# A gated cross-attention block with experts: the last two tiles' steps in another order and on other banks

## The reference

```python
x = x + tanh(g_xattn) * xattn(layernorm(x), ctx, ctx, mask, ...)
x = x + tanh(g_ffn) * ffn(layernorm(x), ...)
# ffn(y):
attn_out = softmax(causal(q @ k.T * scale)) @ v @ out_proj_w.T + out_proj_b
x1 = layer_norm(y + attn_out, ln1_w, ln1_b)                 # "u" in the kernel
gates = softmax(x1 @ gate_w.T + gate_b)
top_gates, top_idx = top 2 of gates
moe_out = sum over the two of gate * (x1 @ expert_w[e].T + expert_b[e])
return layer_norm(x1 + moe_out, ln2_w, ln2_b)               # "v" in the kernel
```

## Time and profile before

| | |
|---|---|
| median of 3 runs | 829.06 us |
| profiled execution, whole | 831.21 us |
| its span from the first to the last instruction | 829.5 us |
| mean granted TensorE clock | 0.994 of 2.4 GHz |
| instructions | 24325 |
| TensorE busy | 779.7 us, 94% of the span |
| VectorE busy | 667.5 us, 80% |
| ScalarE busy | 564.4 us, 68% |
| GpSimd busy | 473.0 us, 57% |

### The profile page before, as it was taken

One profiled execution on the slowest core, in us unless ns is written; L12 is line 12 of the kernel. 1 busy time (PEld: TensorE's weight loads), 2 busy tenths in 40 slices (PEclk: granted clock), 3 DMA queues, 4 the chain that ended last, 5 costly groups with the idle time before them and its releaser, 6 DMA issues.

```text
span 829.5 us, 24325 instructions
## 1 busy us (share of the span) xinstructions
PE 779.7 (94%) x9515; PEld 611.9 (74%) x9515; DVE 667.5 (80%) x1908; ACT 564.4 (68%) x1268; POOL 473.0 (57%) x854
## 2 busy tenths in 40 slices
PE   8888989999999999999999999999999999999896
PEld 4465768777787787778787788778778777777663
DVE  5756668797978979797988979797988979787876
ACT  5786767777786777777776777678677777764320
POOL 8434535566665646566574646566564655555343
PEclk9999999999999999999999999999999999999999
DMA  7510000010100101010100101010010000000000
GB/s 202 159 39 16 2 17 16 8 37 9 37 8 2 37 8 36 9 36 9 29 16 2 38 8 37 8 37 9 10 35 2 9 8 8 9 8 8 8 7 20
DMA packets 33570, 20.75 MB, mean 25 GB/s; under 512 B 11672, under 2 KB 33456, under 8 KB 33456
## 3 DMA queue, kind: packets, MB, share of 16 engines
q1 hardware_dynamic: 33456, 19.19, 8.1%
HBM read 14.99 MB, written 4.19 MB: 23 GB/s over the span
## 4 chain that ended last, share of the span: by engine, by line
PE 56%; ACT 24%; DVE 14%; issue 4%; POOL 1%; DMA 0%; SPq 0%; DVEq 0%; POOLq 0%
PE bank L395 26%; PE bank L516 8%; PE bank L535 7%; ACT bank L776 6%; DVE neg_max_A L1022 6%; ACT bank L785 5%; DVE moe L1131 4%; ACT probs_B L826 3%; PE bank L556 3%; PE bank L585 3%; ACT probs_A L826 3%; PE bank L574 2%; PE bank L404 2%; ACT k_heads_B L809 2%; PE bank L546 1%
## 5 line engine op out<-in xcount | busy, mean ns | idle before, releaser
L1343 POOL TENSOR_SCALAR_AFFINE_SELECT probs_B<-probs_B 128x512 f32<-128x512 f32 x128 | 77.3, 640 | 184.4 <-ACT probs_B L826 184.4
L1131 DVE SCALAR_TENSOR_TENSOR moe<-bank,gates,moe 128x256 f32<-128x256 f32 x256 | 123.2, 481 | 48.2 <-PE bank L395 33.2
L785 ACT ACTIVATE bank<-mask_add 128x512 f32<-128x512 bf16 x128 | 76.6, 602 | 49.2 <-DVE neg_max_A L1022 49.2
L395 PE MATMUL bank<-w_expertsa,u_t_a 128*128 128x512 f32 x256 | 105.6, 413 | 0.1
L395 PE MATMUL bank<-w_expertsa,u_t_b 128*128 128x512 f32 x256 | 100.9, 394 | 0.0
L395 PE MATMUL bank<-w_expertsb,u_t_a 128*128 128x512 f32 x256 | 100.9, 394 | 0.0
L1022 DVE TENSOR_REDUCE neg_max_A<-bank 128x4 f32<-128x512 f32 x128 | 79.5, 684 | 11.9 <-PE bank L516 11.5
L1022 DVE TENSOR_REDUCE neg_max_B<-bank 128x4 f32<-128x512 f32 x128 | 79.3, 682 | 5.5 <-PE bank L516 5.5
L776 ACT ACTIVATE bank<-mask_add 128x512 f32<-128x512 bf16 x128 | 69.8, 626 | 0.0
L776 ACT ACTIVATE bank<-causal_add 128x512 f32<-128x512 bf16 x128 | 69.7, 623 | 0.0
L826 ACT ACTIVATE probs_A<-bank 128x512 f32<-128x512 f32 x128 | 66.1, 603 | 4.4 <-PE bank L556 2.2
(11 more groups left out here) (224 smaller groups left out, 2440.5 us busy)
## 6 DMA issues: line engine op xcount, KB each, us to landing
x_in<-in_x SPq DMA_DIRECT2D x32, 128.0 KB, 2.2
ctx_t<-in_ctxT SPq DMA_DIRECT2D x32, 128.0 KB, 2.2
out<-y_out SPq DMA_DIRECT2D x32, 128.0 KB, 1.7
w_stage<-in_expertsT SPq DMA_DIRECT2D x8, 256.0 KB, 4.3
mask_u<-in_masks SPq DMA_DIRECT2D x32, 32.0 KB, 2.1
w_stage<-in_in_projT SPq DMA_DIRECT2D x3, 256.0 KB, 4.8
w_stage<-in_WkT SPq DMA_DIRECT2D x1, 256.0 KB, 3.5
w_stage<-in_WvT SPq DMA_DIRECT2D x1, 256.0 KB, 3.6
```

Of the source, the lines that this page charges most:

```text
L395: done = pe.matmul(out_ap, l, r, start=n == 0, stop=n == len(terms) - 1)
L785: act.activation(score_banks[g][:].rearrange("p (h k) -> p h k", k=P), mask_add[t % MASK_SLOTS][:, 1:2, :].to_broadcast([P, GROUP, P]), AC ...
L1131: dve.scalar_tensor_tensor(out=moe[(e + 1) % 2][:], in0=bank[:, (e % 2) * EMBED:(e % 2 + 1) * EMBED], scalar=gates[:, e:e + 1], in1=moe[e ...
L1343: pool.affine_select(out=part, in_=part, compare_op=ALU.is_ge, fill=0.0, base=0, pattern=[[0, GROUP], [1, P]], channel_multiplier=-1).then ...
```

## The change

1. A table `LATE` gives six uses of the last tiles a score bank (0 to 3) in place of a work bank: `B_normalise`, `B_o_t`, `B_out`, `u_t` and `gate` of tile 31 and `pair3` of tile 29. They wait for the last exponentials of layer B (`B_exp`), or for nothing more than the steps before them do. `work_last` passes over these uses.
2. `u_transposed` waits for `u` only, in every tile; the wait for its bank's last reader is gone. ScalarE's copy of `u_t` waits, for tiles 30 and 31, for the last expert pair of the tile before.
3. TensorE in round 17: `normalise`, `o_transposed` and `project_o` of tile 31 go in between and behind the pairs of tile 29, five `keep_busy` matmuls go. Round 18: pairs 0 and 1 of tile 30 stand ahead of `transpose_gates(30)`, `u_transposed(31)` ahead of pair 3; `keep_busy` has 6 for 4 and 4 for 8 matmuls.
4. VectorE in round 18: `apply_u(30)`, tile 31's division and `o_t_B_b`, and `u_t_b(30)` go in between the sums of tile 29; the gates of tile 30 go ahead of `statistics("2", 29)`; `statistics("1", 31)` and its mean go into them. `apply_v(29)` goes behind `gates_low(30)`, and `bias_sum(30)` waits for it. Round 19: `u_t_b(31)` goes ahead of the last two sums of tile 30, and the gates of tile 31 ahead of `statistics("2", 30)`.
5. ScalarE takes `B_o_t` of tile 31 ahead of `u_t` of tile 30. GpSimd makes `u` of tiles 30 and 31 ahead of `finish` of tiles 28 and 29.

The diff at its core:

```diff
@@ -235,8 +235,15 @@
         def live(t):
             return 0 <= t < tiles
 
+
+        LATE = {("B_normalise", tiles - 1): (0, "B_exp", GROUPS * tiles), ("B_o_t", tiles - 1): (1, "B_exp", GROUPS * tiles),
+                ("B_out", tiles - 1): (2, "B_exp", GROUPS * tiles), ("pair3", tiles - 3): (3, "B_exp", GROUPS * tiles),
+                ("u_t", tiles - 1): (0, "B_on", tiles), ("gate", tiles - 1): (1, "B_ot_b", tiles)}
+
         def work_bank(use, n):
 
+            if (use, n) in LATE:
+                return score_banks[LATE[use, n][0]]
             key = (use, None) if (use, None) in WORK_AT else (use, n % PAIR)
             return work_banks[WORK_USES[WORK_AT[key]][2]]
 
...
-                _, half, other_bank, behind, readers = WORK_USES[turn % len(WORK_USES)]
+                other, half, other_bank, behind, readers = WORK_USES[turn % len(WORK_USES)]
                 pair = turn // len(WORK_USES) - behind
-                if other_bank == bank and live(PAIR * pair):
+                if other_bank == bank and live(PAIR * pair) and (half is None or (other, PAIR * pair + half) not in LATE):
...
         def tensor_program(pe):
             def take_work(use, t):
+                if (use, t) in LATE:
+                    pe.wait_ge(sem[LATE[use, t][1]], LATE[use, t][2])
+                    return work_bank(use, t)
                 for name, value in work_last(use, t):
                     pe.wait_ge(sem[name], value)
                 return work_bank(use, t)
...
-                transpose_two(take_work("u_t", t), u[t % U_SLOTS], "u_t", t)
+                transpose_two(work_bank("u_t", t), u[t % U_SLOTS], "u_t", t)
...
@@ TensorE, the round's steps
+                if r != 18:
+                    project_o("B", 2 * r - 5)
                 attend("B", 2 * r - 4)
                 scores("A", 2 * r - 1)
                 if r == 18:
-                    keep_busy("gates_t", 30, 4)
+                    keep_busy("gates_t", 30, 6)
+                if r == 18:
+                    expert_pair(0, 2 * r - 6)
+                if r == 18:
+                    expert_pair(1, 2 * r - 6)
                 transpose_gates(2 * r - 6)
-                expert_pair(0, 2 * r - 6)
+                if r != 18:
+                    expert_pair(0, 2 * r - 6)
                 expert_bias_sum(2 * r - 6)
-                expert_pair(1, 2 * r - 6)
+                if r != 18:
+                    expert_pair(1, 2 * r - 6)
                 expert_pair(2, 2 * r - 6)
...
                 normalise("B", 2 * r - 4)
+                if r == 18:
+                    u_transposed(2 * r - 5)
                 expert_pair(3, 2 * r - 6)
                 o_transposed("B", 2 * r - 4)
...
-                    keep_busy("pair0", 31, 8)
+                    keep_busy("pair0", 31, 4)
...
+                if r == 17:
+                    normalise("B", 2 * r - 3)
                 expert_pair(1, 2 * r - 5)
...
+                if r == 17:
+                    o_transposed("B", 2 * r - 3)
...
+                if r == 17:
+                    u_transposed(2 * r - 4)
+                if r == 17:
+                    project_o("B", 2 * r - 3)
                 project_q_b(r - 1)
-                if r == 17:
-                    keep_busy("u_t", 30, 5)
-                normalise("B", 2 * r - 3)
-                u_transposed(2 * r - 4)
+                if r != 17:
+                    normalise("B", 2 * r - 3)
+                if r != 17:
+                    u_transposed(2 * r - 4)
...
+                if use == "u_t" and t >= tiles - 2:
+                    act.wait_ge(sem[read[0]], read[1] * t)
                 act.activation(dst[0][:], work_bank(use, t)[:, 0:EMBED], ACT.Copy).then_inc(sem[name + "_a"], 1)
...
+                if t == tiles - 2:
+                    dve.wait_ge(sem["vn"], t)
...
@@ VectorE, rounds 18 and 19
+                if r == 19:
+                    low_part("u_t", u_t, "u_t", 2 * r - 7)
                 expert_sum(6, 2 * r - 8)
                 apply_x(2 * r - 1)
                 expert_sum(7, 2 * r - 8)
+                if r == 19:
+                    gate(2 * r - 7)
+                if r == 19:
+                    gate_rank(2 * r - 7)
+                if r == 19:
+                    gate_choice(2 * r - 7)
                 statistics("2", 2 * r - 8)
                 mean_variance("2", 2 * r - 8)
                 low_part("B_o_t", o_t["B"], "B_ot", 2 * r - 6)
...
+                if r == 18:
+                    apply_u(2 * r - 6)
                 bias_sum(2 * r - 7)
                 max_parts("A", 2 * r - 2)
                 expert_sum(0, 2 * r - 7)
                 expert_sum(1, 2 * r - 7)
+                if r == 18:
+                    inverse_sums("B", 2 * r - 5)
+                if r == 18:
+                    normalise("B", 2 * r - 5)
                 expert_sum(2, 2 * r - 7)
                 expert_sum(3, 2 * r - 7)
                 if r == 2:
                     split_low("E6")
                     split_low("E7")
                 low_part_of_pair("rope_t", rope_t, "rope_t", 2 * r - 3)
-                apply_u(2 * r - 6)
+                if r != 18:
+                    apply_u(2 * r - 6)
+                if r == 18:
+                    low_part("B_o_t", o_t["B"], "B_ot", 2 * r - 5)
                 expert_sum(4, 2 * r - 7)
                 expert_sum(5, 2 * r - 7)
+                if r == 18:
+                    low_part("u_t", u_t, "u_t", 2 * r - 6)
                 expert_sum(6, 2 * r - 7)
                 expert_sum(7, 2 * r - 7)
+                if r == 18:
+                    gate(2 * r - 6)
+                if r == 18:
+                    finish_b(2 * r - 5)
+                if r == 18:
+                    gate_rank(2 * r - 6)
+                if r == 18:
+                    statistics("1", 2 * r - 5)
+                if r == 18:
+                    mean_variance("1", 2 * r - 5)
+                if r == 18:
+                    gate_choice(2 * r - 6)
                 statistics("2", 2 * r - 7)
                 mean_variance("2", 2 * r - 7)
-                inverse_sums("B", 2 * r - 5)
-                normalise("B", 2 * r - 5)
...
+                if r == 18:
+                    apply_u(2 * r - 5)
                 gates_low(2 * r - 6)
-                mean_variance("1", 2 * r - 5)
+                if r != 18:
+                    mean_variance("1", 2 * r - 5)
                 apply_y(2 * r - 2)
                 maxima("A", 2 * r - 1)
+                if r == 18:
+                    apply_v(2 * r - 7)
                 bias_sum(2 * r - 6)
                 expert_sum(0, 2 * r - 6)
                 expert_sum(1, 2 * r - 6)
...
@@ GpSimd, round 19
+                if r == 19:
+                    scale_shift_u(2 * r - 8)
                 finish(2 * r - 10)
                 base_b(2 * r - 7)
-                scale_shift_u(2 * r - 8)
+                if r != 19:
+                    scale_shift_u(2 * r - 8)
...
```

More of the change, by code:

```diff
@@ L1159, in vector_program @@
                 low_part("y_t", y_t, "y_t", 2 * r - 5)
-                low_part("u_t", u_t, "u_t", 2 * r - 7)
+                if r != 19:
+                    low_part("u_t", u_t, "u_t", 2 * r - 7)
                 maxima("B", 2 * r - 5)
@@ L1221, in vector_program @@
                 apply_x(2 * r)
-                low_part("u_t", u_t, "u_t", 2 * r - 6)
-                apply_v(2 * r - 7)
-                low_part("B_o_t", o_t["B"], "B_ot", 2 * r - 5)
+                if r != 18:
+                    low_part("u_t", u_t, "u_t", 2 * r - 6)
+                if r != 18:
+                    apply_v(2 * r - 7)
+                if r != 18:
+                    low_part("B_o_t", o_t["B"], "B_ot", 2 * r - 5)
                 mean_variance("A", 2 * r + 1)
@@ L1233, in vector_program @@
                 mean_variance("B", 2 * r - 2)
-                gate_rank(2 * r - 6)
-                gate_choice(2 * r - 6)
-                finish_b(2 * r - 5)
+                if r != 18:
+                    gate_rank(2 * r - 6)
+                if r != 18:
+                    gate_choice(2 * r - 6)
+                if r != 18:
+                    finish_b(2 * r - 5)
                 if r == 0:
@@ L1240, in vector_program @@
                 low_part_of_pair("x_t", xn_t, "xn", 2 * r)
-                statistics("1", 2 * r - 5)
+                if r != 18:
+                    statistics("1", 2 * r - 5)
+                if r == 18:
+                    apply_u(2 * r - 5)
                 gates_low(2 * r - 6)
-                mean_variance("1", 2 * r - 5)
+                if r != 18:
+                    mean_variance("1", 2 * r - 5)
                 apply_y(2 * r - 2)
                 maxima("A", 2 * r - 1)
+                if r == 18:
+                    apply_v(2 * r - 7)
                 bias_sum(2 * r - 6)
@@ L1250, in vector_program @@
                 expert_sum(2, 2 * r - 6)
-                apply_u(2 * r - 5)
+                if r != 18:
+                    apply_u(2 * r - 5)
```

(5 more changed lines are left out.)

28 lines of the change are left out of this document (20 added, 8 removed).

## The result

| | before | after |
|---|---|---|
| median, same chip | 829.14 us (829.02 to 831.9, 7 runs) | 832.37 us (831.01 to 833.45, 7 runs) |
| ratio | | 1.0032 (95% interval 1.0021 to 1.0043) |
| profiled execution, span | 831.21, 829.5 | 832.29, 830.6 |
| granted clock in it | 0.994 | 0.996 |

What follows compares the result with a forecast made beforehand. TensorE, 94% busy, bounds the middle; the last 20 us are a chain of waits through GpSimd, VectorE and TensorE. Tile 31's bias matmul moves from 817.63 to 818.21, so 829.06 + 0.58 = 829.6 us; range 827.3 to 831.4.

Steps and rivals of the forecast that it cites:

- v_n: VectorE's apply_v(30) ahead of gates_low(31), meeting GpSimd's addition: 0.73 us taken, 0.40 with GpSimd quiet.
- Cost one: TensorE, tile 29: transposes directly behind the bias matmul wait for ScalarE's copy; 1.05 us, of which 0.47 only moved.
- Cost two: Ahead of tile 30's bias matmul: two GpSimd roots in a row, 1.69 us, leave TensorE 1.8 us idle.
- Cost three: Tile 30's statistics, mean, root and apply_v ahead of gates_low(31): last bias matmul at 818.21 against 817.63.
- The early gates: VectorE's gates of tile 31 were to come at 815.67 against 816.56, 0.9 us early.
- The parts priced at nothing: Wait taken from u's transposes (0 taken, 2.8 us at most), bank addresses, idle matmuls, ScalarE's added wait: no effect.
- The first, early gates carrying through: Rival: apply_v(30) doesn't hold gates_low and the end is 828.2, or 826.5 to 827.4 with the issue; chance 0.27.
- The second, the clock: Rival: TensorE's clock halves behind the new waits of 1.8 and about 1.4 us; 830.6, 831.0 or 832; chance 0.23.
- The third, nothing seen: Rival: losses some tenths smaller cancel with the gain, 829.1; within the forecast's own spread, 828.9 to 830.3.

Runs made afterwards that it cites:

- before filled more: Kernel before with two pairs of idle matmuls in TensorE's waits near 800 and five more near 746.7: 829.1 us, ratio 0.9989.
- the run with 15 waits: Changed kernel with both statistics moved back, TensorE's waits filled, plus 15 met semaphore waits in VectorE's tile 20: 830.85 us, ratio 1.0013.
- the filled kernels: Kernels with idle matmuls in TensorE's waits, among them before with two pairs (829.16 us), before with five more (829.1), the changed kernel (831.14).

## Why the prediction was wrong, point by point

**The step that failed** is the first sentence of the sum: "It is made on the span's axis of the profiled execution (829.5 us of its 831.21) and put on the median, 829.06, as a difference." The old order stood in it with a half-clock stretch inside the compared piece (tile 29 to tile 30: 13.44 us, 793.78 to 807.22), the new one at full clock (13.89 reckoned, 13.99 in the trace). At full clock the old one takes 12.18, and as far as tile 31's bias matmul 22.73 where the forecast had 23.85. So the difference of the first piece was put at 0.45 and is 1.80. I had the row that shows it and used it for a rival, not for the baseline. The 2.2 us between the profiled execution and the median were the same hint, two steps of 1.1. The end of that piece in the trace of before:

```profile
807.22 0.28 PE L611 MATMUL bank<-expert_bias,gates_t 128*128 128x256 f32 x1
```

The forecast's 829.64 thus lacks 1.12 for the baseline, 0.14 for the way to the last bias matmul (24.43 reckoned, 24.57 in the changed kernel's trace at full clock) and 0.23 for the hole behind it: 831.1, where the changed kernel has 831.0 at full clock. The other 1.3 us of the measured 832.37 are the clock again: that run was at 0.996, a step lower, while the median of before lay on its best step.

**The new order's events were right.** Predicted and measured on the trace after: transposes of o_raw 794.6 and 794.69; u(30) 799.63 and 799.68; TensorE's wait 1.8 and 2.05; bias matmul of tile 30 807.67 and 807.89; u(31) 809.3 and 809.51; end of tile 31's gates 815.67 and 815.82; v_n 0.73 behind a wait of 0.95 and 1.02; last bias matmul 818.2 and 818.49. Every sign that was named came in that trace (full clock behind 794 us too, though most runs of this kernel are at 0.996 or less), and none of them could tell that the baseline was off.

**Cost one** was 1.05, of which 0.47 moved; the 0.61 that stay in the table are near the 0.58 that don't move, but no run took it away alone, so this is argued and not shown. **Cost two** was 1.69 of stall; taken away it is worth 1.19, since the statistics then stand ahead of the gates (0.56). **Cost three** was called the one that decides ("So of a gain of 0.9 a loss of 0.58 is made"). It decided little: taken away it gives 0.4, because the gates move back by 1.2. The early gates had no gain of 0.9 to lose either, that too was the old order's half clock. At full clock the last step of tile 31's gates starts 21.43 us behind tile 29's bias matmul in the old order and 21.67 in the new one, so 0.24 later (before filled more, then the changed kernel):

```profile
814.08 0.23 DVE L1113 TENSOR_SCALAR gates<-chosen,gate_inv 128x24 f32<-128x24 f32 x1
```

```profile
814.25 0.23 DVE L1142 TENSOR_SCALAR gates<-chosen,gate_inv 128x24 f32<-128x24 f32 x1
```

**The parts priced at nothing**: right for the waits ahead of u's transposes (0.9996). What was left out is the added semaphore wait, called by no name in the forecast: 0.2.

**v_n** beside GpSimd's addition ends at 818.12, 0.15 after the addition (817.97). By the rule of the Trainium skill, "SBUF — State Buffer", section "Who interferes with whom", that the second blocks fully behind the first, it would end at 818.37. So 0.73 was the right size, as forecast, and not 0.25 more. In the casts of the run with 15 waits the rule fits better: the first, 0.18 long by itself, ended 0.06 behind the GpSimd operation. GpSimd's times in a profile are rough, so a tenth proves little here.

**The rivals.** The first, early gates carrying through, did not come. The second, the clock, came in part of the runs: 15 of the changed kernel's 19 lie on a lower step, and filling its waits left 2 of 11 there. But before has such stretches too (65 of 116 at 0.996 or less), so over many runs the clock adds only some 0.3 us to the 2.0 (medians 832.4 of 19 and 830.1 of 116). In the result, with seven runs of each, it added 1.2 to the distance of the medians. The Trainium skill, "TensorE: Matmul & The Clock Gate", section "What's actually happening", has work releasing the clock, so that idle time is itself a price; the filled kernels agree, as idle matmuls alone took before from 830.0 to 829.1. Whether the clock falls behind a wait differs from run to run of one program, which no row explains. The third, nothing seen, fell with the baseline.

**The range** ended at 831.4. With the right baseline the forecast would have been 829.1 + 0.58 + 1.12 (the 23.85 less 22.73), 830.8 at full clock, and its upper end two steps of 1.1 higher, 833.0.

## What to carry to other kernels

Before a ledger is put on a median, look at the granted clock of both: a profiled execution 2 us over the median is not the execution that the median stands for, and a half-clock stretch inside the compared piece must be taken out of the old order as well. Lay two traces at the same clock against each other, in distances between the same instructions. A step moved ahead of another's statistics also moves what GpSimd has in its queue and what VectorE meets beside it; the price is that queue's, not the instruction's.

## What the runs showed of the hardware

- A stretch of 3.4 us at half clock (1.2 of 2.4 GHz) costs this kernel about 1.1 us each time, and the times stand in steps of it (829.1, 830.2, 831.3). Which runs have it varies. With five idle matmuls in a wait of 1.27 us near 746.7 and four in two waits near 801, none of 11 runs lay on a lower step (829.0 to 829.8).
- One semaphore wait that was already met put a hole of 0.46 us into VectorE's program a tile behind it, at the third of the last eight sums. With 15 such waits the holes stood elsewhere, and the times were 1.1 and 1.4 us longer.
- Some VectorE operations took longer where their rows lie beside GpSimd's: a comparison of 64 columns 0.75 for 0.23, a cast 0.72 for 0.18, v_n 0.61 and 0.73 for 0.40.
